# Nine empty products instead of seven on TensorE at the start, and two more between the two groups of transposes

## What is computed

```python
g = jnp.einsum('bsd,edf->ebsf', h, Wg)
u = jnp.einsum('bsd,edf->ebsf', h, Wu)
expert_outs = jnp.einsum('ebsf,efd->ebsd', jax.nn.silu(g) * u, Wd)
expert_output = jnp.einsum('be,ebsd->bsd', gating_probs, expert_outs)
shared = jnp.einsum('bsf,fd->bsd', jax.nn.silu(h @ Sg) * (h @ Su), Sd)
x = x + (1.0 - sg) * expert_output + sg * shared
```

## Time and profile before

| | us |
|---|---|
| median of 3 runs | 163.94 |
| lowest and highest of the 3 | 163.27 and 164.56 |
| span of the profiled execution | 161.7 |
| TensorE busy in it | 155.3 (96%) |
| ScalarE busy | 109.8 (68%) |
| VectorE busy | 99.0 (61%) |
| GpSimd busy | 76.3 (47%) |

### The profile page before, as it was taken

The page is one execution under the profiler, slowest core; times in us unless marked ns, Lnnn a source line. Parts: engine busy times, 40 slices in busy tenths (PEclk is TensorE's granted clock), DMA queues, the critical chain, the costliest instruction groups (busy, mean ns, idle before and its releaser), DMA issues.

```text
span 161.7 us, 2332 instructions
## 1 busy us (share of the span) xinstructions
PE 155.3 (96%) x674; PEld 125.8 (78%) x674; DVE 99.0 (61%) x157; ACT 109.8 (68%) x203; POOL 76.3 (47%) x77
## 2 busy tenths in 40 slices
PE   7599999999999999999999999999999999999991
PEld 2378888888888888888888888888888888888860
DVE  0449766666666666666666566666666666666751
ACT  3368886686668766776687668766876687655541
POOL 4069878255725572557354735473547354400000
PEclk9999999999999999999999999999999999999998
DMA  5946006000600050006000600050000000000004
GB/s 116 249 163 192 3 0 195 4 0 4 195 0 0 6 191 4 0 0 192 3 0 0 192 2 0 0 183 11 0 0 0 0 0 0 0 0 0 0 0 130
DMA packets 9525, 8.22 MB, mean 51 GB/s; under 512 B 544, under 2 KB 7200, under 8 KB 9520
## 3 DMA queue, kind: packets, MB, share of 16 engines
q1 hardware_dynamic: 9312, 7.87, 15.5%
q10 hardware_dynamic: 144, 0.26, 0.9%
q0 software_dynamic: 64, 0.04, 0.8%
HBM read 7.64 MB, written 0.52 MB: 50 GB/s over the span
## 4 chain that ended last, share of the span: by engine, by line
PE 93%; DMA 3%; DVE 1%; issue 1%; DVEq 0%; POOLq 0%
PE y_ps L488 10%; PE y_ps L483 10%; PE y_ps L485 10%; PE u_ps L558 9%; PE g_ps L553 9%; PE g_ps L555 9%; PE g_ps L554 9%; PE u_ps L560 9%; PE u_ps L559 9%; DMA sg_sb<-in_condB_sharedgateprob 3%; PE g_ps L499 1%; PE g_ps L501 1%; PE g_ps L503 1%; PE u_ps L513 1%; PE u_ps L515 1%; PE u_ps L517 1%
## 5 line engine op out<-in xcount | busy, mean ns | idle before, releaser
L413 DVE TENSOR_TENSOR h_ps<-silu,u_ps 128x512 f32<-128x512 f32 x71 | 49.4, 696 | 50.8 <-PE u_ps L560 45.7
L314 ACT ACTIVATE h_hi<-h_ps 128x512 fp32r<-128x512 f32 x71 | 42.6, 600 | 39.7 <-DVE h_ps L413 39.7
L247 POOL TENSOR_TENSOR w_lo<-w_raw,w_hi 128x384 fp32r<-128x384 f32 x32 | 32.6, 1017 | 39.1 <-ACT w_hi L299 39.1
L419 DVE TENSOR_TENSOR h_lo<-h_ps,h_hi 128x512 fp32r<-128x512 f32 x71 | 48.6, 684 | 0.1
L306 ACT ACTIVATE silu<-g_ps 128x512 f32<-128x512 f32 x72 | 43.0, 597 | 0.3 <-PE g_ps L503 0.3
L252 POOL TENSOR_TENSOR xs_lo<-xs,xs_hi 128x512 fp32r<-128x512 f32 x16 | 20.7, 1291 | 16.3 <-ACT xs_hi L295 16.3
L488 PE MATMUL y_ps<-h_lo,w_hi 128*128 128x512 f32 x71 | 27.6, 389 | 0.0
L483 PE MATMUL y_ps<-h_hi,w_lo 128*128 128x512 f32 x71 | 27.6, 389 | 0.0
L485 PE MATMUL y_ps<-h_hi,w_hi 128*128 128x512 f32 x71 | 27.6, 389 | 0.0
L554 PE MATMUL g_ps<-x_lo,w_hi 128*128 128x512 f32 x64 | 24.9, 389 | 0.0
L558 PE MATMUL u_ps<-xs_hi,w_hi 128*128 128x512 f32 x64 | 24.9, 389 | 0.0
(11 more groups left out here) (61 smaller groups left out, 123.5 us busy)
## 6 DMA issues: line engine op xcount, KB each, us to landing
w_raw<-in_L_cond_Wg SPq DMA_DIRECT2D x8, 256.0 KB, 2.8
w_raw<-in_L_cond_Wu SPq DMA_DIRECT2D x8, 256.0 KB, 3.1
w_raw<-in_L_cond_Wd SPq DMA_DIRECT2D x8, 256.0 KB, 3.5
x_nat<-in_x SPq DMA_DIRECT2D x2, 256.0 KB, 6.0
out<-out_sb SPq DMA_DIRECT2D x2, 256.0 KB, 2.3
w_raw<-in_L_cond_Sg ACTq DMA_DIRECT2D x1, 256.0 KB, 3.6
w_raw<-in_L_cond_Su SPq DMA_DIRECT2D x1, 256.0 KB, 4.5
w_raw<-in_L_cond_Sd SPq DMA_DIRECT2D x1, 256.0 KB, 5.2
```

The source lines that it names most:

```text
L314: act.activation(h_hi[k % HB][:, :], h_ps[k % BANKS][:, :], ACT.Copy)\
L413: dve.tensor_tensor((to or h_ps[k % BANKS])[:, :], silu[k % BANKS][:, :], u_ps[k % BANKS][:, :], ALU.mult).then_inc(hidden_done, 1)
L419: dve.tensor_tensor(h_lo[k % HB][:, :], h_ps[k % BANKS][:, :], f32(h_hi[k % HB][:, :]), ALU.subtract).then_inc(h_lo_done, 1)
```

## The change

The first row of empty products grows from seven to nine, and two more are put between the first and the second transposes. All of them write `g_ps[1]`, as before.

```diff
-WARM_UP = 7
+WARM_UP = 9
+WARM_BETWEEN = 2
...
             pe.wait_ge(zeros_set, 1)
-            for _ in range(WARM_UP):
-                pe.matmul(g_ps[1][:, :], zeros[:, 0:P], zeros[:, :], start=True, stop=True)
+            def warm(n):
+                for _ in range(n):
+                    pe.matmul(g_ps[1][:, :], zeros[:, 0:P], zeros[:, :], start=True, stop=True)
+
+            warm(WARM_UP)
             pe.wait_ge(ident_built, 1)
...
             pe.wait_ge(x_loaded[0], DMA)
             transpose(x_nat, y_ps[0], 0, x_transposed)
+            warm(WARM_BETWEEN)
             pe.wait_ge(xs_nat_done, 1)
             transpose(xs_nat, h_ps[0], 0, xs_transposed)
```

## The result

| | before | after |
|---|---|---|
| median, us | 163.86 (16 runs) | 162.72 (16 runs) |
| lowest to highest | 162.60 to 164.98 | 162.61 to 163.16 |
| span of the profiled execution | 161.7 | 161.0 |

The ratio is 0.9929, with a 95% interval of 0.9912 to 0.9946: 0.7% faster. The median falls by 1.1 us, and the spread from 2.4 to 0.55 us. The lowest run is the same. So the change doesn't make the best case better. It made each of these 16 executions a good one.

A forecast was written before the change was run, and what follows sets the result against it. TensorE was taken as the bound, its early products at 1.2 GHz until about 10.6. An early rise saves 1.26 us: span 161.7 to 160.4, median 163.94 to 162.68, lowered to 162.4 for run scatter; range 161.6 to 164.0.

The forecast's parts named there:

- Parts 1 and 2: Two more empty products before the first transposes, two between the transposes: both fit TensorE's idle time, cost nothing, at most 0.86 us each.
- Part 3: TensorE's rise to 2.4 GHz comes before the second transposes at 7.29, not at about 10.6; gain 1.26 us.
- The size of the gain behind the second transposes: Third transposes start at 10.82 instead of 12.08, after stalls of 0.3 and 0.08 us: 1.26 us gained.
- the stall in up unit 1: Up unit 1 would read GpSimd's slices 1 to 3 at 10.51 but starts at 10.59: 0.08 us.
- Given back further on: Routed expert 0 starts at 23.6 instead of 24.84, its last input done at 20.15; TensorE bounds from there, span 160.4 us.
- From the span to the median: Median 162.68 us if the profiled execution is typical, 162.0 if it is the quickest kind; 162.4 taken between.
- R1: Rival: TensorE's clock rise comes early only in some executions, median 163.2 us; chance 0.20.
- R2: Rival: empty products of zeros don't raise TensorE's clock level, or not in time, 163.9 us; chance 0.16.
- R3: Rival: products between delay the second transposes if the gate's transfer lands early, 164.8 us far case, 164.2 middling; chance 0.07.
- The rule on transposes: The Trainium skill's rule that TensorE's transpose-mode work isn't counted as busy and doesn't bring the full clock; would give 163.2 us.

## Why the prediction was right, point by point

The forecast was 162.4 us, between 161.6 and 164.0, most likely within 1%; 162.72 came, 0.7% less than before.

**Parts 1 and 2, cost nothing: right.** The second transposes waited for VectorE alone, 1.28 us in the profile after. The first ones started at 5.01 right behind the ninth product; if the tokens landed a little earlier, the 0.8 us of slack behind them took it, since nothing of it shows in the sum of the table.

**Part 3, the rise comes before 7.29: right,** in the profile (5.7) and, going by the spread of 0.55 us and mean clocks of 0.995 and more, in all 16 runs. The argument for it was too simple. I set 3.85 us without a pause against the 3.3 us before the rise in the trace of before, and asked only when the level rises. Nine in a row without the two between gave the gain in a quarter of the runs only, and by the mean clocks the level did rise in eight of the others and was lost. The two parts together raise it and keep it.

**The size of the gain behind the second transposes: 1.26 forecast, 1.07 measured.** The way from the second to the third transposes was to take 3.53 us and took 3.72. The mis-sized term is what a product costs that had to wait. The forecast puts down its wait, and then 0.23 us to the next start. In the profile after, the third product of gate unit 0 waits as forecast (8.87, 8.62 if nothing held it; 1.21 us behind the second transposes, 1.18 forecast), but the next one starts 0.33 later, at 9.20. That is 0.10 of the 0.19 us. The other steps up to the first up product (9.90, 2.24 behind the second transposes, 2.09 forecast) add 0.05.

The rest, 0.04, is the stall in up unit 1. GpSimd's slices were to hold its last product up by 0.08 us. GpSimd starts at 9.56, 1.90 behind the second transposes and not 1.85. The product starts on time at 11.05, but here too the next start is 0.33 later (11.38). The view of GpSimd's line names who waited for it (total us, times), the load of that product's weights:

```profile
  PEld u_ps L521: 0.3, 1
```

ScalarE's take-up of the second transposes was 0.70 behind their start, 0.64 forecast, and that is why GpSimd began later. (The prediction's 0.16 us from 7.73 would give 7.89; its 7.93 is the value that it goes on with.)

**Given back further on: nothing, right.** From the third transposes to the end it is 161.7 - 12.08 = 149.6 us before and 161.0 - 11.38 = 149.6 after. L558 starts at 24.14 with the second transposes at 7.66. With these at 7.29, as in the forecast, it would be 23.8 (23.6 forecast). The span would be 160.6 and not 160.4; the second profile of the changed kernel has 7.30 and a span of 160.6.

**From the span to the median: this step failed by its shading.** I took the profiled execution of before as typical, which gives 162.68, and then went down to 162.4, in case it were one of the quick ones. It needed no shading. The time is 1.76 us above the span (162.76 and 161.0), so that execution took about 163.5 us, 0.4 us under the median. An execution at the median of before has more to win than this one had. Against that, the second transposes of the profiled execution after started 0.37 us later, and by the table they vary from 7.04 to 7.72 in any kernel. Added up, 0.4 more, 0.37 less and the 0.19 above nearly cancel out, and the unshaded 162.68 is 0.04 from the measured 162.72. That it is so close is luck. That the spread would shrink I had not put in numbers at all.

**The rivals.** R1 (only some executions) is what the nine alone do, and one run of the 28 of the changed kernel. R2 (products of zeros don't raise the clock) is wrong for the changed kernel, and by the mean clocks for the seven of before too. What the prediction named as its own breaking point, that the seven did raise the level in most runs, is half true: they did in about half of them. It broke nothing, since the level was lost again ahead of the work that needed it, and the time to be won was still there (164.14 without any, 164.21 with them). R3 (the products between are in the way): never seen, with four of them neither.

But R3's sentence that a fall of the level in the pauses is no danger was wrong, and it is the real miss of this prediction: this fall is what the two between keep off. I took 0.35 us as the longest pause. It follows from the lower level; once the clock is up the two products are short and the pause is 1.3 us in the profile after, and 2.8 us in one execution of another kernel, where the level did fall.

**The rule on transposes** was weighed rightly: the rows of before spoke against it, and the kernel with transposes between decided against it.

## What to carry to other kernels

Empty products at the start pay only if the level that they bring is kept up to the first real work: seven in a row were worth nothing, the same seven with two in a later pause 1.3 us. Fill the pauses first, then lengthen the row. Look at the spread of the runs and at the mean granted clock of each, and not only at the median or at one profile: a clock that rises and falls again shows there. Once the clock is up, the start is bound by the transfers that land first; holding later loads back was worth 0.5 us here.

## What was not expected of the hardware

- A granted clock of 1.00 in the profile doesn't prove the higher level at the start: the column read 1.00 while products started 0.43 us apart, with the earlier trace rows. The distance of the starts tells it.
- The clock fell back to 0.50 at 8.1, 2.1 us into a pause of 2.8, and came back only at 14.9, about 6 us after work had resumed at 8.82.
- In 38 of 77 executions of the kernel before the mean clock (0.990 or less) says that the level rose, fell and rose again; without a first row it was 0 of 36.
- Four float32 transposes between held the gain like two products (162.91 against 163.95 us with nothing).
- VectorE's product of 128x512 with GpSimd active beside it took 1.44 us, not 0.69, and a small one (128x64) 1.37, not 0.31.
- A product that had waited was followed by the next after 0.33 us, not 0.23 (8.87 to 9.20).
- A 4 KB transfer put ahead on ScalarE's queue went with gate weights used at 6.01, not 4.38, and down weights used at 10.14.
